# A gated graph network on one Trainium2 core: both pairs of chunks get gates of seven products, and the queues around them are put in another order

## The reference

```python
for _ in range(5):
    a_in  = A   @ (state @ in_W.T  + in_b)
    a_out = A.T @ (state @ out_W.T + out_b)
    a = concat([a_in, a_out, state])
    r = sigmoid(a @ r_W.T + r_b)
    z = sigmoid(a @ z_W.T + z_b)
    h = tanh(concat([a_in, a_out, r * state]) @ h_W.T + h_b)
    state = (1 - z) * state + z * h
out = tanh(state @ o1_W.T + o1_b) @ o2_W.T + o2_b
return layernorm(x + out)
```

## Time and profile before

| what | value |
|---|---|
| median of three runs | 1040.41 us (1038.47 to 1041.48) |
| profiled execution | 1037.02 us |
| its span | 1035.2 us |
| instructions in the span | 11766 |
| mean granted TensorE clock | 0.987 |
| PE, DVE, ACT busy | 993.9, 666.0, 425.4 us |

### The profile page before, as it was taken

How to read it: one execution, slowest core, us unless ns; L and a number is a source line. 1 busy time by engine, 2 the same in 40 slices (tenths; PEclk the granted TensorE clock), 3 DMA queues, 4 the chain that set the end, 5 groups by cost and what they waited for, 6 DMA issues and landing times.

```text
span 1035.2 us, 11766 instructions
## 1 busy us (share of the span) xinstructions
PE 993.9 (96%) x4576; PEld 450.9 (44%) x4576; DVE 666.0 (64%) x1052; ACT 425.4 (41%) x594; POOL 35.3 (3%) x43
## 2 busy tenths in 40 slices
PE   7999999998999999999999999999999999977995
PEld 3444444443444444444444444444444444433443
DVE  5999968995884348467634765763367477516756
ACT  3666565541453226334412643341255245302443
POOL 0311000000000000000000000000000000002100
PEclk9999999998999999999999999999999999998998
DMA  9999991334610543462045247402534650141101
GB/s 345 386 396 407 379 290 31 77 82 117 183 41 2 161 123 72 92 183 82 1 122 148 62 72 188 123 1 82 158 70 84 155 163 2 41 148 41 41 1 41
DMA packets 199110, 134.32 MB, mean 130 GB/s; under 512 B 61712, under 2 KB 191376, under 8 KB 194960
## 3 DMA queue, kind: packets, MB, share of 16 engines
q1 hardware_dynamic: 196752, 125.20, 41.6%
q0 software_dynamic: 2304, 8.39, 2.1%
HBM read 102.11 MB, written 16.78 MB: 115 GB/s over the span
## 4 chain that ended last, share of the span: by engine, by line
PE 79%; DVE 12%; ACT 3%; issue 3%; DMA 2%; SPq 1%; POOL 0%; ACTq 0%; DVEq 0%; POOLq 0%
PE bank L1499 31%; PE bank L1597 24%; PE bank L1610 10%; PE bank L1625 6%; PE bank L1441 5%; DMA areg<-in_x 2%; ACT areg L636 1%; PE bank L1687 1%; PE bank L1668 1%; DVE scal L829 1%; DVE xop_words L806 1%; DVE w L839 1%; DVE pq_words L963 0%; DMA xop_words<-pq_words 0%; DVE areg L1215 0%
## 5 line engine op out<-in xcount | busy, mean ns | idle before, releaser
L1499 PE MATMUL bank<-areg,xop_words 128*128 128x512 fp8e4 x1792 | 395.2, 382 | 18.4 <-DVE pq_words L1188 13.3
L1499 PEld LDWEIGHTS bank<-areg,xop_words 128*128 128x128 f16 x1792 | 175.2, 98 | 236.0 <-DVE pq_words L1188 15.8
L636 ACT ACTIVATE areg<-pq_words 128x512 f16<-128x512 f32 x72 | 45.4, 630 | 237.0 <-DVE pq_words L1181 118.4
L1597 PE MATMUL bank<-areg,w 128*128 128x512 f16 x576 | 131.0, 379 | 0.0
L1441 PE MATMUL bank<-areg,xop_words 128*128 128x512 fp8e4 x512 | 112.3, 379 | 3.5 <-ACT areg L484 3.2
L540 ACT ACTIVATE tmp<-bank,bias_sb,scal 128x512 f32<-128x512 f32 x72 | 55.8, 775 | 104.1 <-PE bank L1597 104.1
L1597 PEld LDWEIGHTS bank<-areg,w 128*128 128x128 f16 x576 | 56.4, 98 | 68.0 <-DVE areg L1215 0.2
L1441 PEld LDWEIGHTS bank<-areg,xop_words 128*128 128x128 f16 x512 | 49.4, 98 | 65.8 <-issue 7.4
L484 ACT ACTIVATE areg<-tmp 128x2048 fp8e4<-128x2048 int32 x32 | 61.1, 1910 | 39.9 <-DMA tmp<-in_adj_t 21.0
L1597 PE MATMUL bank<-split,w 128*128 128x512 f16 x288 | 70.0, 379 | 2.4 <-issue 1.9
L1215 DVE SCALAR_TENSOR_TENSOR areg<-pq_words,areg 128x512 f16<-128x512 f32 x72 | 49.8, 692 | 32.7 <-ACT areg L636 31.9
(11 more groups left out here) (178 smaller groups left out, 1007.8 us busy)
## 6 DMA issues: line engine op xcount, KB each, us to landing
areg<-kept_operands SPq DMA_DIRECT2D x112, 512.0 KB, 4.3
tmp<-in_adj SPq DMA_DIRECT2D x16, 1024.0 KB, 7.2
tmp<-in_adj_t SPq DMA_DIRECT2D x16, 1024.0 KB, 8.0
kept_operands<-xop_words POOLq DMA_DIRECT2D x11, 512.0 KB, 8.2
areg<-in_x SPq DMA_DIRECT2D x8, 512.0 KB, 6.9
kept_operands<-areg SPq DMA_DIRECT2D x4, 1024.0 KB, 9.7
kept_operands<-tmp POOLq DMA_DIRECT2D x5, 512.0 KB, 3.3
pq_words<-in_gate_w SPq DMA_DIRECT2D x6, 384.0 KB, 5.4
```

The source lines that it names most:

```text
L636: nc.scalar.activation(y_dst(g, name)[:, 0, :], src, ACT.Copy, scale=PSC).then_inc(s_yh, 1)
L1499: last = nc.tensor.matmul(dst[:, :], xop[:, m // 2, operand_block(xo, part, m % 2), :], place8[:, mo, m, :], start=first and m == pairs[0] ...
L1597: last = nc.tensor.matmul(dst[:, :], w16[:, k, wp, feat(gi)], rhs, start=False, stop=i == KT - 1 and (wp, xp) == PASSES[-1], skip_group_ch ...
```

## The change

- Chunks 2 and 3 of steps 1 to 3 become a pair as well (`paired`); in step 4 they keep the plain gates. All pair functions get an argument p, and `degd` a second array for the differences of degrees.
- The second and third gate of a pair go through their tiles in the order 1, 2, 0, 3. Other banks hold the tiles.
- P7 and P4 go to bank f (the eighth). PE's waits follow: P7 waits for y21 of the group before, P6 for the sum that reads P6 of the group before. The sums are made in other buffers, with one addition less.
- `first_group` of steps 2 to 4 begins with chunks 0 and 1 alone (in step 1 with 0 to 2), has parts of P3 and P7 among the early products, and takes chunks 3 and 2, in this order of arrival, late.
- Chunks 0 and 1 are turned after the first pair's gates and in group 3, chunks 3 and 2 at the end of the step, interleaved with the last updates.
- Three of the four seeds of a pair's first gate are made ahead of the pair's first group, the fourth in its second group.
- In step 1 the cast and the low half of the first weights' sums move behind P1's copy and behind `sums_v` of group 0.
- In step 4 SP issues the bias and x for chunks 0 and 1 ahead of the operands of groups 1 to 3. `head_out` uses other banks and `head_hidden` of chunk 1 waits for the residual of chunk 0.

```diff
+PAIR_ORDER = ((0, 1, 2, 3), (1, 2, 0, 3), (1, 2, 0, 3))
+TURN_ORDER = {False: (0, 1, 2, 3), True: (0, 1, 3, 2)}
...
-        h_pair = (sum_1, sum_u, sum_v, sum_u)
+        h_pair = (sum_v, sum_1, sum_u, sum_u)
...
-        pair_banks = (bank[4:8], (bank_a, bank_b, bank_e, bank_c), bank[4:8])
+        pair_banks = ((bank[4], bank[5], bank[6], bank_b), (bank_c, bank_a, bank_e, bank_f),
+                      (bank[4], bank[5], bank[6], bank_b))
...
+        def paired(t, g):
+            return g < 2 or t < LAST
...
+        def turn_parts(t):
+            ns = range(CH * t, CH * (t + 1))
             if t == 0:
+                return [(n, f) for n in ns for f in range(FT)]
+            return [(ns[0], 0), (ns[0], 1), (ns[1], 0), (ns[1], 1), (ns[2], 0), (ns[3], 0), (ns[2], 1), (ns[3], 1)]
...
@@ SP
             for t in range(1, STEPS):
+                if t == LAST:
+                    sp.wait_ge(s_xl, 2 * CH * LAST)
+                    sp.dma_start(b2_all, o2_b.partition_broadcast(P)).then_inc(s_b2, 16)
+                    load_rest(0)
+                    load_rest(1)
                 for at in range(4 * (t - 1) + 1, 4 * t + 1):
                     if at < 4 * LAST:
                         load_group(at)
                 if t < LAST:
-                    for c in range(CH):
-                        turn_rows(CH * t + c)
-
-            sp.wait_ge(s_xl, 2 * CH * LAST)
-            sp.dma_start(b2_all, o2_b.partition_broadcast(P)).then_inc(s_b2, 16)
...
+                    turn_rows(t)
...
@@ ACT, group(t, g)
                 copy_p1(t, g)
-                if g == 1:
-                    for i in range(4):
-                        pair_seed(t, 0, i)
...
+                if t == 1 and g == 0:
+                    weight_hi(0)
...
+                if paired(t, g) and g == 3:
+                    rows_hi(CH * t + 1, 0)
+                if paired(t, g) and g % 2:
+                    pair_seed(t, g // 2, 0, 3)
+                if paired(t, g) and g == 3:
+                    rows_hi(CH * t + 1, 1)
...
@@ ACT, end of pair_gates(t, p)
+                pair_act(t, p, 2, 0)
+                pair_act(t, p, 2, 1)
+                if p == 1:
+                    rows_hi(CH * t + 2, 0)
+                pair_act(t, p, 2, 2)
+                pair_act(t, p, 2, 3)
+                if p == 1:
+                    rows_hi(CH * t + 3, 0)
+                    rows_hi(CH * t + 2, 1)
+                    rows_hi(CH * t + 3, 1)
...
@@ DVE
-            def sums_v(at):
+            def sums_v(t, g):
+                at = 4 * (t - 1) + g
                 dve.wait_ge(s_p5, at + 1)
-                nc.vector.tensor_tensor(sum_v, bank_e[:, :], sum_1, ALU.add).then_inc(s_sumv, 1)
                 dve.wait_ge(s_sumu, at + 1)
-                nc.vector.tensor_tensor(sum_u, bank_e[:, :], sum_u, ALU.add).then_inc(s_u4, 1)
+                nc.vector.tensor_tensor(sum_v, bank_e[:, :], sum_u, ALU.add).then_inc(s_u4, 1)
...
@@ DVE, group(t, g)
+                if g == 0:
+                    y_lo(t, g, "y11")
+                sums_v(t, g)
+                if t == 1 and g < 2:
+                    weight_sums(1) if g else weight_lo(0)
+                if paired(t, g) and g == 3:
+                    rows_lo(CH * t + 1, 1)
                 y_sum(t, g, "y22")
                 y_lo(t, g, "y22")
                 y_sum(t, g, "y12")
...
@@ DVE, end of pair_gates(t, p)
+                pair_update(t, p, 0)
+                pair_update(t, p, 1)
+                if p == 1:
+                    rows_lo(CH * t + 2, 0)
+                    row_sums(CH * t + 2)
+                pair_update(t, p, 2)
+                pair_update(t, p, 3)
+                if p == 1:
+                    rows_lo(CH * t + 3, 0)
+                    row_sums(CH * t + 3)
+                    rows_lo(CH * t + 2, 1)
+                    rows_lo(CH * t + 3, 1)
...
@@ DVE, the loop of steps
-                    weight_lo(0)
+                for s in range(3):
+                    pair_degree(t, 0, 0, s)
                 group(t, 0)
                 split_lo(0, split_at(t, 0))
                 split_lo(1, split_at(t, 1))
                 group(t, 1)
-                pair_gates(t)
...
+                pair_gates(t, 0)
+                if t < LAST:
+                    rows_lo(CH * t, 0)
+                    row_sums(CH * t)
+                    rows_lo(CH * t, 1)
+                    for s in range(3):
+                        pair_degree(t, 1, 0, s)
+                    group(t, 2)
+                    split_lo(2, split_at(t, 2))
+                    split_lo(3, split_at(t, 3))
+                    group(t, 3)
+                    pair_gates(t, 1)
...
@@ PE, group(t, g)
                 product(bank_a, at, X11, M11, every).then_inc(s_p1, 1)
-                need(pe, s_y21, at)
+                pe.wait_ge(s_sumu, at)
                 if g == 2:
-                    pe.wait_ge(s_zh, FT * CH * t + 2)
+                    pe.wait_ge(s_act, GT * pair_at(t, 0) + 12)
                 product(bank_b, at, XS2, MT2, every).then_inc(s_p6, 1)
...
-                pe.wait_ge(s_sumu, at + 1)
-                product(bank_b, at, XS3, MT3, every, first=False).then_inc(s_p7, 1)
+                pe.wait_ge(s_y21, at)
+                if g == 2:
+                    pe.wait_ge(s_zh, zs + 4)
+                product(bank_f, at, XS3, MT3, every).then_inc(s_p7, 1)
...
@@ PE, first_group(t)
+                early, late = (range(6), (6, 7)) if t == 1 else (range(4), (6, 7, 4, 5))
+                wait_turned(pe, 0, n - len(late) // 2)
...
+                product(bank_c, at, XS4, M22, early, final=False)
+                if t > 1:
+                    pe.wait_ge(s_zh, zs + 4)
+                product(bank_f, at, XS3, MT3, early[:-2], final=False)
                 wait_turned(pe, 0, n)
                 product(bank_a, at, X11, M11, late, first=False).then_inc(s_p1, 1)
+                product(bank_f, at, XS3, MT3, early[-2:], first=False, final=False)
                 pe.wait_ge(s_sum1, at + 1)
                 product(bank_a, at, X12, M21, every, first=False).then_inc(s_p2, 1)
                 wait_turned(pe, 1, n)
                 product(bank_b, at, XS2, MT2, late, first=False).then_inc(s_p6, 1)
                 product(bank_e, at, XS1, MT1, late, first=False).then_inc(s_p5, 1)
+                product(bank_f, at, XS3, MT3, late, first=False).then_inc(s_p7, 1)
                 product(bank_c, at, XS4, M22, late, first=False).then_inc(s_p3, 1)
                 pe.wait_ge(s_y22, at + 1)
+                product(bank_f, at, X22, MT4, every, first=False).then_inc(s_p4, 1)
...
@@ PE, pair_gate(t, p, gate)
+                for s in PAIR_ORDER[gate]:
+                    if s == 0:
+                        pe.wait_ge(s_gs1, unit + 1)
+                        pair_product(t, p, gate, slots[0], "y21", block(0, 1))
+                    elif s == 1:
+                        pe.wait_ge(s_g12, unit + 1)
+                        pair_product(t, p, gate, slots[1], "y22", block_sum(4))
+                    elif s == 2:
+                        pe.wait_ge(s_g22, unit + 1)
+                    else:
+                        pe.wait_ge(s_g21, unit + 1)
+                        pair_product(t, p, gate, slots[3], "t4", block(1, 1))
+                    pair_state(t, p, gate, s)
...
@@ PE, the loop of steps
                 group(t, 3)
-                gates(t, 2)
-                gates(t, 3)
+                if t < LAST:
+                    for gate in range(3):
+                        pair_gate(t, 1, gate)
+                else:
+                    gates(t, 2)
+                    gates(t, 3)
```

More of the change, by code:

```diff
@@ L245, in pair_term, with y_order @@
-        def pair_term(gate, i, d):
-            return ((deg[:, d, cols(0)], vdeg[:, d, FT * gate:FT * gate + 1]),
-                    (degd[:, d, :], vdif[:, d, 0, gate:gate + 1]),
-                    (degd[:, d, :], vdeg[:, d, FT * gate + 1:FT * gate + 2]),
-                    (deg[:, d, cols(1)], vdif[:, d, 1, gate:gate + 1]))[i]
+        def paired(t, g):
+            return g < 2 or t < LAST
+        def y_order(t, g):
+            if g == 0:
+                return "y11", "y22", "t1", "t3", "t2", "y21", "t4"
+            return ("y22", "t3", "y11", "t1", "t2", "y21", "t4") if paired(t, g) else ("y22", "y12", "y11", "y21")
@@ new lines, in y_before, with y_dst, y_sum_at @@
+        def y_before(t, g):
+            return sum(len(y_order(i // 4 + 1, i % 4)) for i in range(4 * (t - 1) + g))
+        def y_done(t, g, name):
+            return y_before(t, g) + y_order(t, g).index(name) + 1
+        def y_dst(t, g, name):
+            if paired(t, g):
+                return yop[:, g % 2, Y_PLACE[name], :, :]
+            return pq_late[:, int(name[2]) - 1, FT * (1 - g % 2) + int(name[1]) - 1, :, :]
+        def y_sum_at(g, name):
+            return {"t1": sum_b if g == 0 else sum_v, "t2": sum_a if g == 0 else sum_b,
```

(36 more changed lines are left out.)

610 lines of the change are left out of this document (315 added, 295 removed).

## The result

The changed kernel takes 1004.2 us (median of 4, 1003.08 to 1006.11) against 1039.44 for the kernel before on the same chip: ratio 0.9664, interval 0.9636 to 0.9692. On a second chip the ratio was 0.9687 (0.9671 to 0.9704). Forecast was 1007, from 33.4 us of gain. The profiled execution has a span of 1002.2 us. The first fence is the page's busy line of the changed kernel, the second its waits of PE (us in total, times, longest).

What follows compares the result with a forecast made beforehand. The prediction took the number of matrix products on PE as the bound, plus a few PE waits. Gains 11.7 - 1.3 + 2.7 + 7.5 + 12.8 = 33.4 us took 1040.4 to 1007.0 us, range 1002 to 1017.

Steps and rivals of the forecast that it cites:

- The gates: Gates of chunks 2 and 3, steps 1-3: 198 products instead of 216, 54 fewer in all, 11.7 us gained.
- Rival E: New pair not cheaper, as VectorE can't keep up in it; 12.4 us eats the 11.7: 1019 us, chance 0.05.
- The step end: Three step ends: PE waits about 0.45 us each for the second large transpose, 1.3 us lost.
- no wait over 1 us: Sign that the forecast is right: PE has no wait over 1 us in steps 2 and 3.
- the bound of 2 us for the landing: Step ends: stall of 2 us each if one transpose's landing takes a microsecond and a half more.
- B: Turn much later: PE waits 3 us or more at three step ends, then half clock: 1023 us, chance 0.06.
- D: Slower than before: PE stands at the last turn's second part, from 9.7 us waits; 1047 at 11; chance 0.03.
- A bank of its own for P7: Steps 2-4: P7 and P4 in their own bank remove small PE waits for P6's sum and y21, 2.7 us gained.
- The weights: Step 1: P1's copy no longer delays PE, a new 1.8 us wait for y22 appears; 7.5 us gained together.
- The load of x: Step 4: x loaded at the step's start removes the 11.1 us wait and 1.7 at half clock, 12.8 us gained.
- the 5.5 us that the prediction drew from it as the most: Step 4: by the shared-port rule VectorE could lose all 5.5 us of GpSimd's additions, sum up to 3.9 worse.
- C: Last step's wait moves: late operand loads, head_hidden(1) or seeds hold PE; 1016 us, chance 0.09.

Runs made afterwards that it cites:

- x_late: The changed kernel with the bias and x for the residual issued behind all operand loads again in step 4: 1012.91 us, ratio 0.9765.

## Why the prediction was right, and where it was not

**1. The gates.** Right in size and in kind. 54 products less is in the page; the stage in which no other term of the sum lies gained the 3.88 us forecast, the second pair of step 1 takes the 42.7 us of its products, and putting the same number back cost 3.89 a step. The pair has no wait, but only by a third of a microsecond: I had estimated 0.4, the additions measured 0.36. Rival E fell.

**2. The step end.** The mechanism was right and its size off: 2.3 us of listed waits, 2.8 with the 0.17 beside each (1.17, 1.13 and 0.54 us), in place of 1.3. One was 1.01, just over the sign "no wait over 1 us". VectorE and ScalarE were as worked out (large transposes issued at T+6.0 and T+9.8, forecast 6.2 and 9.3; PE asks at T+13.8). The mis-sized term is SyncE's time for the first large transpose, taken at 3.0 from one row and measured at 3.7 at two of three ends. I gave the bound of 2 us for the landing and none for the issue, though one transpose of the old trace, near the end of step 2, also held SyncE for 3.6:

```profile
609.93 3.59 SPq L390 DMA_TRANSPOSE xop_words<-pq_words  x1
```

That the total came out is luck in part: this term is 1.5 us worse and the next 1.3 better. B and D need waits of 3 and 9.7 us; they fell. (655 KB in 3.01 us is 218 GB/s, not 215; nothing hangs on it.)

**3. A bank of its own for P7.** More than the 2.7 us came. The gain of steps 2 and 3 and of step 4 up to group 2 is 8.93 us. Of it 7.77 are the products of steps 2 and 3, and 2.8 were lost at the step ends, so the small waits gave 4.0. The listed waits, of which the 2.7 was made, left out the 0.17 beside each of the six, which is most of the difference. The reason given was "P7 no longer waits for the sum of P6 (L1168), and P6 of the next group no longer for y21". The runs don't show this as the cause: with the wait of P6 for y21 put back nothing was lost, and with the order of VectorE alone, in the old banks, both waits went, for 3.4 of the 4.0. I took the waits that the edit deletes as the cause and did not look at which operations VectorE now does sooner. The bank alone, in the old order, was not run; there y21 would first be needed at P7, 32 products behind P6, so it may have been enough too. With the order in place the bank has two other uses that I did not price: it lets P6 run while y21 is late (3.5 us of cover in step 4, unused while x is early), and it lets `first_group` begin P7 before P6 is summed. The second was not tried by itself.

**4. The weights.** Right: 7.65 of 7.5 (6.1 of 6.2 in the groups, 1.5 of 1.3 in the pair), the new wait cost 1.8 of 1.8 (1.66 listed), and the clock stayed at 1.00 behind it.

**5. The load of x.** Right: 12.95 of 12.8, and alone it is worth as much. No operand came late. The additions of GpSimd ran beside VectorE at 800.15 to 806.93, and the two slowed each other: one addition of VectorE took 1.02 us for 0.69, and a pair of low halves 1.81 for 1.48, 0.7 in all, while PE waited for neither. The slower ones, t3's sum (L1267) and low halves (L1290), have both inputs in SBUF; sums with an input in a bank (L1275 at 804.54) took their 0.69 beside the same additions. The Trainium skill ("SBUF — State Buffer", "SBUF: two separate sides") says that VectorE's operations with two SBUF inputs and GpSimd's that read SBUF take turns at a shared pair of ports, a whole instruction at a time. The trace agrees in kind, but of the 5.5 us that the prediction drew from it as the most, 0.7 came. As to C, half of it is true in `x_late`: late residual rows would now hold the hidden layer.

```profile
803.29 3.64 POOL L511 TENSOR_TENSOR areg<-areg,diag_words 128x256 f32<-128x256 f32 x4 [0.36 <-DMA areg<-in_x]
...
804.54 0.69 DVE L1275 TENSOR_TENSOR pq_words<-pq_words,bank 128x512 f32<-128x512 f32 x1
...
805.33 1.02 DVE L1267 TENSOR_TENSOR pq_words<-pq_words 128x512 f32<-128x512 f32 x1
806.27 1.81 DVE L1290 SCALAR_TENSOR_TENSOR areg<-pq_words,areg 128x512 f16<-128x512 f32 x2
```

The forecast was 2.8 us above the measured time; 1.0 of it is the lower base (1039.44 for 1040.41), and the rest is within the spread of the runs. The sum itself, 33.4 us, stands against 33.0 between the two spans and 35.2 between the medians.

## What to carry to other kernels

Where one engine is busy 96% of the span, its saved instructions can be priced by count, and the rest of a change by walking each wait from the operation that ends last; that gave 33.3 us for 33.4 here, with two terms off by 1.5 and 1.3 in opposite directions. Price a wait from product start to product start, as the listed wait leaves out 0.17 us each time. When an edit removes a wait, look as well at what it moves in the queue of the engine that was waited for: the order there may be enough by itself. For transfers issued back to back from one queue count the time that each holds the queue, and take it from all rows of its kind, not from one.

## What the runs showed of the hardware

- A large DMA transpose (20 blocks of 128x128, two bytes) held SyncE for 2.98 to 4.54 us with the same code and data sizes (2.98 to 3.88 as the first large one of a step end in the changed kernels), and landed 4.8 to 6.6 us after its issue.
- A product of 128x512 started 0.2158 us after the one before, but 0.17 us more than the listed wait was lost whenever PE had waited.
- VectorE's operations with two inputs in SBUF took up to 1.02 for 0.69 us beside GpSimd's additions; those with an input in PSUM kept 0.68 to 0.69.
- Waits of PE of 1.0, 1.7 and 1.9 us left its granted clock at 1.00. Behind those of 3.3 (the last head), 3.9, 6.2 and 11 us it was 0.66, 0.57, 0.53 and 0.50. Behind the 3.9 the same 24 products took 8.04 us in one profile and 7.04 in another.
- The first product of step 1 started at 230.4 to 233.8 us in the fourteen profiles, of kernels that do the same work up to there. The 2.1 us between medians of the kernel before on different chips is within that. The same stages behind it agree to some 0.3 us, other than behind a long wait.
